# Quantised stage of a three-layer kernel: squares kept in the gelu's low half, and both streams' first rows turned before the first product

## The reference, cut to what matters

```python
def _qlora_linear(x, q, scale, bias, la, lb):
    w = _dequant(q, scale)
    base = jnp.einsum('btd,od->bto', x, w) + bias
    lora = jnp.einsum('btr,or->bto', jnp.einsum('btd,rd->btr', x, la), lb)
    return base + lora
h = x
for blk in range(3):
    i0, i1 = (2 * blk, 2 * blk + 1)
    y = _qlora_linear(h, qweights[i0], scales[i0], biases[i0], lora_a[i0], lora_b[i0])
    y = _layernorm(y, ln_gamma[blk], ln_beta[blk])
    y = jax.nn.gelu(y, approximate=False)
    y = _qlora_linear(y, qweights[i1], scales[i1], biases[i1], lora_a[i1], lora_b[i1])
    h = y + h
...
x = _layernorm(x + _L0_ffn_ref(x, ...), axis=-1)
```

## Time and profile before

| | us |
|---|---|
| median of 3 runs | 2350.44 (2347.72 to 2354.53) |
| the profiled execution, its own time | 2346.15 |
| its span, first to last instruction | 2344.4 |
| mean granted TensorE clock in it | 0.985 |

### The profile page before, as it was taken

The page is one execution under the profiler, slowest core; times in us unless marked ns, Lnnn a source line. Parts: engine busy times, 40 slices in busy tenths (PEclk is TensorE's granted clock), DMA queues, the critical chain, the costliest instruction groups (busy, mean ns, idle before and its releaser), DMA issues.

```text
span 2344.4 us, 35695 instructions
## 1 busy us (share of the span) xinstructions
PE 2249.4 (96%) x11839; PEld 1876.6 (80%) x11839; DVE 1494.6 (64%) x2746; ACT 1277.6 (54%) x2449; POOL 693.6 (30%) x993
## 2 busy tenths in 40 slices
PE   7999999998699999999999999999999999999997
PEld 6999999997578777778787787877877788888886
DVE  3666666676565665666666567566566766666666
ACT  4455555555545354354463444535445577777775
POOL 2565555665100100101001010010010235555555
PEclk9999999998899999999999999999999999999999
DMA  5122221235101102002011020110210423333322
GB/s 146 55 99 89 98 104 51 103 136 155 59 1 55 54 1 90 18 18 72 18 54 54 18 72 18 54 54 0 89 49 19 160 73 108 107 107 107 107 90 72
DMA packets 101704, 166.12 MB, mean 71 GB/s; under 512 B 19664, under 2 KB 22480, under 8 KB 101520
## 3 DMA queue, kind: packets, MB, share of 16 engines
q1 hardware_dynamic: 97328, 163.69, 20.5%
q10 hardware_dynamic: 4320, 1.71, 0.3%
HBM read 115.05 MB, written 50.33 MB: 71 GB/s over the span
## 4 chain that ended last, share of the span: by engine, by line
PE 52%; DVE 11%; ACT 5%; DMA 3%; issue 2%; POOL 1%; DVEq 0%; POOLq 0%; ACTq 0%
PE quant_bank L2002 6%; PE quant_bank L2004 6%; PE quant_bank L2003 6%; PE quant_bank L1631 5%; PE quant_bank L1632 4%; PE quant_bank L1633 4%; PE quant_bank L1661 3%; PE quant_bank L1662 3%; PE quant_bank L1663 3%; DMA x_d<-quant_y 3%; DVE quant_g_lo L1551 2%; DVE quant_h_lo L1512 2%; PE quant_bank L1682 2%; PE quant_bank L1684 2%; PE quant_bank L1683 2%
## 5 line engine op out<-in xcount | busy, mean ns | idle before, releaser
L1429 POOL TENSOR_TENSOR quant_up_rstd<-quant_up_var,quant_minus_half 128x4 f32<-128x4 f32 x48 | 48.6, 1012 | 916.5 <-DVE quant_up_var L1539 916.5
L1631 PE MATMUL quant_bank<-quant_h_hi,kept_W_hi 128*128 128x512 f32 x768 | 308.0, 401 | 7.1 <-DVE quant_h_lo L1512 7.1
L1632 PE MATMUL quant_bank<-quant_h_hi,kept_W_lo 128*128 128x512 f32 x768 | 304.3, 396 | 0.0
L1633 PE MATMUL quant_bank<-quant_h_lo,kept_W_hi 128*128 128x512 f32 x768 | 304.2, 396 | 0.0
L1468 ACT ACTIVATE quant_y<-quant_bank,quant_b_root 128x512 f32<-128x512 f32 x192 | 127.3, 687 | 296.1 <-DMA x_d<-quant_y 158.3
L1967 DVE TENSOR_TENSOR mlp_g_lo<-quant_bank,mlp_g_hi 128x512 fp32r<-128x512 f32 x256 | 176.4, 689 | 106.8 <-ACT quant_bank L1904 106.7
L1903 ACT ACTIVATE mlp_g_hi<-quant_bank,mlp_b 128x512 fp32r<-128x512 f32 x256 | 177.4, 693 | 71.6 <-PE quant_bank L2004 63.7
L1661 PE MATMUL quant_bank<-quant_g_hi,kept_W_hi 128*128 128x512 f32 x512 | 209.0, 408 | 0.0
L1662 PE MATMUL quant_bank<-quant_g_hi,kept_W_lo 128*128 128x512 f32 x512 | 203.6, 398 | 0.0
L1663 PE MATMUL quant_bank<-quant_g_lo,kept_W_hi 128*128 128x512 f32 x512 | 203.3, 397 | 0.0
L1525 DVE TENSOR_TENSOR quant_y<-quant_y 128x512 f32<-128x512 f32 x96 | 66.5, 693 | 212.5 <-ACT quant_y L1468 211.5
(11 more groups left out here) (309 smaller groups left out, 5846.9 us busy)
## 6 DMA issues: line engine op xcount, KB each, us to landing
delta_x_in<-L_attn_x_d SPq DMA_DIRECT2D x16, 1024.0 KB, 8.2
delta_x_res<-L_attn_x_d SPq DMA_DIRECT2D x16, 1024.0 KB, 5.6
x_d<-delta_z SPq DMA_DIRECT2D x64, 256.0 KB, 2.1
quant_y<-x_d SPq DMA_DIRECT2D x16, 1024.0 KB, 5.1
x_d<-quant_y SPq DMA_DIRECT2D x16, 1024.0 KB, 4.2
mlp_x_in<-x_d SPq DMA_DIRECT2D x16, 1024.0 KB, 10.3
mlp_x_res<-x_d SPq DMA_DIRECT2D x16, 1024.0 KB, 6.6
out_d<-mlp_z SPq DMA_DIRECT2D x15, 1024.0 KB, 8.7
```

Source lines behind the costliest of these rows:

```text
L1631: mm(tr[j][:, :], W_hi[2 * b][:, k, cols], h_hi[m][:, k, :], start=k == 0, stop=False)
L1632: mm(tr[j][:, :], W_lo[2 * b][:, k, cols], h_hi[m][:, k, :], start=False, stop=False)
L1633: last = mm(tr[j][:, :], W_hi[2 * b][:, k, cols], h_lo[m][:, k, :], start=False, stop=k == KT - 1)
```

## The change

Three things are changed, all in the quantised layer.

1. The squares get a place of their own, `sq[m]`, which is the memory of `g_lo[m]`. `square`, `part` and both `total` pieces use it instead of `y[m]`. The wait for `x_out` moves from ACT's `square` to DVE's `normed`, the first piece that now writes `y[m]` in a step.
2. In step 0 all `enter` pieces, of both streams, come first on every engine. Stream 1's rows go into the three `lin` banks and `shared` (`first_banks`), so they don't wait for stream 0's `normed`; `up` of stream 1 waits for it instead. The first `total` on PE and the first `down` wait for stream 1's `h_lo`, since they write those banks.
3. ACT's work on the biases moves from the start of the layer to behind the eighth `enter`, with `y[1]` as scratch, and DVE waits for it only before the first `normed`.

```diff
+        sq = [placed(nc, f"quant_sq{m}", [P, KT, R], F32, g_at + (2 * m + 1) * size_of([P, KT, R])) for m in range(STREAMS)]
...
+        first_banks = lin + [shared]
...
-            for what, m, b, i, behind in order:
+            first_enters = several("enter", 0, 0, KS) + several("enter", 1, 0, KS)
+            for what, m, b, i, behind in first_enters + [piece for piece in order if piece not in first_enters]:
...
+        def ahead(t, m):
+
+            return isinstance(t, int) and (t, m) == (0, 1)
+
+        def enters_in(t, m):
+
+            return first_banks if ahead(t, m) else tr
...
+            def centred_biases():
...
-                nc.scalar.activation(h_hi[m][:, k, :], tr[k][:, :], ACT.Copy).then_inc(s["h_hi_done"], 1)
+                nc.scalar.activation(h_hi[m][:, k, :], enters_in(t, m)[k][:, :], ACT.Copy).then_inc(s["h_hi_done"], 1)
+                if isinstance(t, int) and (t, m, k) == (0, 1, KT - 1):
+                    centred_biases()
...
-                if b == 0 and j == 0:
-                    wait(act, s["x_out"], 16 * t)
-                nc.scalar.activation(y[m][:, j, :], tr[j][:, :], ACT.Square, bias=b_root[:, b, j:j + 1], scale=ROOT).then_inc(s["sq_done"], 1)
+                nc.scalar.activation(sq[m][:, j, :], tr[j][:, :], ACT.Square, bias=b_root[:, b, j:j + 1], scale=ROOT).then_inc(s["sq_done"], 1)
...
-            dve.wait_ge(b_done, 2 * BLOCKS)
...
-                nc.vector.tensor_tensor(y[m][:, 0, :], y[m][:, 0, :], y[m][:, j, :], ALU.add).then_inc(s["part_done"], 1)
+                nc.vector.tensor_tensor(sq[m][:, 0, :], sq[m][:, 0, :], sq[m][:, j, :], ALU.add).then_inc(s["part_done"], 1)
...
                     dve.wait_ge(s["row_done"], BLOCKS * t + b + 1)
+                    if b == 0:
+                        wait(dve, s["x_out"], 16 * t)
+                        if isinstance(t, int) and (t, m) == (0, 0):
+                            dve.wait_ge(b_done, 2 * BLOCKS)
...
-                else:
+                elif not ahead(t, m):
                     pe.wait_ge(S[0]["normed"], KT * BLOCKS * t + k + 1)
...
-                if 0 in ks and m == 1 and b > 0:
+                if 0 in ks and m == 1 and (b > 0 or ahead(t, m)):
                     pe.wait_ge(S[0]["normed"], KT * (BLOCKS * t + b) + j + 1)
...
                 pe.wait_ge(s["sum_done"], BLOCKS * t + b + 1)
+                if isinstance(t, int) and (t, m, b) == (0, 0, 0):
+                    pe.wait_ge(S[1]["h_lo_done"], KT)
...
                     lin_free(pe, t, "down", m, b, j)
+                    if isinstance(t, int) and (t, m, b) == (0, 0, 0):
+                        pe.wait_ge(S[1]["h_lo_done"], KT)
```

More of the change, by code:

```diff
@@ L1446, in _ @@
         def _(act):
[L1447 to L1454, removed]
+            def centred_biases():
+                for b in range(BLOCKS):
+                    nc.scalar.activation(y[1][:, b, :], b_all[:, b, :], ACT.Copy, scale=-1.0 / dim, accum_out=b_mean[:, b:b + 1]).then_inc(b_done, 1)
+                act.wait_ge(b_done, BLOCKS)
+                for b in range(BLOCKS):
+                    nc.scalar.activation(b_mid[:, b, :], b_col[:, 2 * b, :], ACT.Identity, bias=b_mean[:, b:b + 1]).then_inc(b_done, 1)
+                act.wait_ge(b_done, 2 * BLOCKS)
+                nc.scalar.activation(b_root[:, :, :], b_mid[:, :, :], ACT.Copy, scale=ROOT).then_inc(b_done, 1)
+                act.wait_ge(b_done, 2 * BLOCKS + 1)
             def enter(t, m, b, k):
@@ L1516, in enter @@
                     dve.wait_ge(S[m]["xT_ps"], KT * t + KT)
-                split_h(t, m, 0, k, tr[k][:, :])
+                split_h(t, m, 0, k, enters_in(t, m)[k][:, :])
             def part(t, m, b, j):
@@ L1532, in total @@
                 dve.wait_ge(s["part_done"], 2 * u + 2)
-                nc.vector.scalar_tensor_tensor(y[m][:, 0, :], y[m][:, KT - 1, :], LN_EPS / P, y[m][:, 0, :], ALU.add, ALU.add).then_inc(s["sum_done"], 1)
+                nc.vector.scalar_tensor_tensor(sq[m][:, 0, :], sq[m][:, KT - 1, :], LN_EPS / P, sq[m][:, 0, :], ALU.add, ALU.add).then_inc(s["sum_done"], 1)
             def spread(t, m, b, _):
@@ L1613, in enter @@
                     wait(pe, S[1]["normed"], KT * (BLOCKS * t - 1) + k + 1)
-                else:
+                elif not ahead(t, m):
                     pe.wait_ge(S[0]["normed"], KT * BLOCKS * t + k + 1)
                 for r in range(RT):
-                    last = nc.tensor.transpose(tr[k][:, r * P:(r + 1) * P], arrived(t, m)[:, r, k * P:(k + 1) * P], ident)
+                    last = nc.tensor.transpose(enters_in(t, m)[k][:, r * P:(r + 1) * P], arrived(t, m)[:, r, k * P:(k + 1) * P], ident)
                 last.then_inc(s["xT_ps"], 1)
@@ L1639, in total @@
                 pe.wait_ge(s["sum_done"], BLOCKS * t + b + 1)
+                if isinstance(t, int) and (t, m, b) == (0, 0, 0):
+                    pe.wait_ge(S[1]["h_lo_done"], KT)
                 for r in range(RT):
-                    last = nc.tensor.transpose(by_rows[:, r, :], y[m][:, 0, r * P:(r + 1) * P], ident)
+                    last = nc.tensor.transpose(by_rows[:, r, :], sq[m][:, 0, r * P:(r + 1) * P], ident)
                 last.then_inc(s["sum_ps"], 1)
```

## The result

| | before | changed |
|---|---|---|
| median us | 2349.08 (4 runs, 2347.04 to 2354.53) | 2310.68 (4 runs, 2310.04 to 2311.67) |
| ratio, 95% interval | | 0.9833 (0.9816 to 0.9851) |
| span of the profiled execution | 2344.4 | 2309.9 |

The changed kernel is faster by 1.7%: 38.4 us by these medians, 34.5 us by the two profiled spans. A second set of 19 runs of the kernel before gave 2347.49, 36.8 us above the changed kernel. The forecast was 2313 in 2305 to 2322.

The account below looks back on a forecast made before the run. PE, busy 96% of the span, was taken as the bound. Gains 27.6 + 4.5 + 3.4 - 0.4 = 35.1 us gave 2311.1 from the profiled 2346.15, or 2315.3 from the median; forecast 2313, range 2305 to 2322.

Parts of the forecast that it names:

- What bounds the kernel: Whole kernel: PE is busy 96% of the span, so other engines' waits count only as far as they reach PE.
- The stalls: PE at `total`, 14 places in steps 1 to 7: idle time and pipe filling all go, 27.6 us, lower bound 20.6.
- the clock behind them: PE behind three of the stalls: stretches at the lower clock go, 1.5 us each, 4.5 us; lower bound 0.
- the new wait: DVE ahead of the first `normed` of a step: the added wait instruction costs 0.03 us each, 0.4 us in 14.
- the halfway correction: Forecast time: median runs 4.3 us above the profiled execution; the middle of 2311.1 and 2315.3 was taken, 2313.
- The moved wait: DVE's `normed`, step 1: the store lands before DVE needs it, 7.0 us to spare for stream 0, some 6 for stream 1.
- The first pass: Step 0: `up` of stream 1 starts 3.4 us earlier (bounds 2.2 and 3.9), `up` of stream 0 1.3 us later.
- a term set at nothing: Step 0, `up` of stream 1: slow matmuls at 1.2 GHz before and after set against each other, 1.5 us either way.
- moving the biases: ACT, start of the quantised layer: biases end near 626.5, ahead of the first square; moving them costs nothing.
- part of the stall stayed: Rival, PE at `total`: DVE's sum comes late, 19 us gained, 2327 to 2331; chance 0.05.
- other wait took its place: Rival: PE waits elsewhere for the same time, only the first pass gained, 2343 to 2347; chance 0.02.
- The one that ends slower: Rival, DVE's `normed`: stores landing beyond 11.2 us hold it; gain eaten up at 13.7 us, 2366 at 15; chance 0.03.

Follow-up runs that it names:

- the wait back: Changed kernel with only the wait for the store put back on ACT's first square of a step and taken from DVE, squares staying in `g_lo`: 2345.64 us.
- squares alone: Kernel before with only the squares moved to `g_lo` and the store wait on DVE's `normed`; order and first pass as before: 2314.08 us.
- biases first: Changed kernel with ACT's nine bias instructions back ahead of its first `enter` copy, DVE's early wait staying away: 2310.67 us.
- the store after the fourth square: Changed kernel with each store of steps 0 to 6 issued only after the fourth square of the next step's first block: 2310.39 us.
- The delayed stores: Changed kernel with stores of steps 0 to 6 held until the next step's fourth square, `total` or `spread`: 2310.39, 2315.47, 2361.36 us.
- the first pass alone: Changed kernel with squares, sums and the store wait back in `y`, keeping the new first pass and moved biases: 2344.44 us.
- the stores held back to `spread`: Changed kernel with each store of steps 0 to 6 issued only after PE's `spread` of the next step's first block: 2361.36 us.

## Why the prediction was right

**What bounds the kernel.** The reading held. 158.3 us of ACT's wait were worth 33 us, because only what reached PE counted: the kernel with the wait back has ACT's wait and PE's, and is as slow as before.

**The stalls, 27.6 us, and the clock behind them, 4.5 us, less 0.4 for the new wait.** Together 31.7; the stretch with the seven steps is 32.5 us shorter, and squares alone gave 33.4 between medians. Of the 32.5, 24.7 us are PE's idle time at `total`, as read the earlier trace rows, and 7.8 are what the prediction had as pipe filling and clock, 7.4. The clock of 0.87 and 0.88 behind three of the stalls is gone: the window of the changed kernel from 700 to 1740 us reads 1.00. That every stall would go was argued from two rows where `total` had no wait; the distance at the same place is now 0.59 us, like the 0.60 of the unstalled block. That the clock term varies between runs is borne out by the runs: 19 of the kernel before spread over 9.4 us, the fastest (2342.89) at a mean granted clock of 0.989, the slowest (2352.32) at 0.983. Twelve runs without the stalls, of the changed kernel, of biases first and of the store after the fourth square, spread over 3.0 us (2309.16 to 2312.11). The price of 1.5 us for each stretch was read at one of the three; the other two have fewer slow matmuls (5 and 6, not 8). The step "the median of before lies above its profile, and that difference goes too" was a choice between 2311.1 and 2315.3; the sum made against the profiled execution, 2311.1, was the better one, and the halfway correction an addition that the result didn't need. The range's gain of 29 to 39 us was narrower than the bounds set for the terms (20.6 for the stalls and 0 for the clock at the low end), so that the measured gain lies inside it says little for the low end.

**The moved wait.** Put at 7.0 us to spare for stream 0 and some 6 for stream 1. In step 1 of the changed kernel the stores land 7.1 and 5.3 us before `normed` (773.38 + 4.17 against 784.65, 800.02 + 5.11 against 810.43). The delayed stores bear out the size: nothing lost at 4.6 us, 4.8 us at about 6.6. Stream 1 has the less room, because its `normed` follows a `down` and came 810.43 - 803.60 = 6.8 us after the last matmul of `up`, where stream 0's came 784.65 - 776.85 = 7.8 after it; the prediction had used stream 0's distance for both. The term of 0.4 us for the wait instruction itself was a guess that no row of before showed, and it didn't reach PE. On DVE it can be read: from the end of ACT's `rstd_row` to the first `normed` of stream 0 it is 0.13 to 0.14 us in steps 1 to 7, where the kernel before has 0.03; for stream 1 it is 0.03 in both.

The section from which the prediction takes its 4.4 us for a store (the Trainium skill, DMA: Bandwidth & Descriptors, "Anatomy of one DMA — SWDGE (gpsimd) path") is about transfers issued from GpSimd. These stores are issued from SyncE, so that they land in 4.2 us at the median is no test of it. The rule that a transfer's completion can come surprisingly late when its target is HBM (the Trainium skill, Perfetto Trace Analysis, "DMA Instruction — HWDGE (DVE, Sync)") did not show here: the stores land in 4.1 to 5.1 us in the changed kernel.

**The first pass, 3.4 us.** 3.2 in the trace, 3.1 between medians without the squares and 3.4 with them, but that the sum behind it came out was partly luck. `up` of stream 1 starts 22.79 us into the layer where it started at 27.12, 4.3 us earlier, since `up` of stream 0 came only 0.7 us later (5.11 for 4.45), not 1.3: about half of the 32 transposes started 0.21 us apart, as all 16 had before, and the other half 0.11 us apart, which makes some 1.8 us for the second sixteen where 2.3 had been taken. Against that stands a term set at nothing, with 1.5 us either way: 13 matmuls of that `up` ran at 1.2 GHz, where it had been 7. Before, 16 transposes had run in the slow stretch ahead of the matmuls; now the matmuls themselves, which are longer, are in it. Six more, 0.2 us each, are 1.2 us. This varies too: the seven traces with the new first pass up to the delayed stores have 9 to 13 such matmuls. That moving the biases would cost and give nothing held exactly (2310.67 for 2310.68).

**The rivals.** No part of the stall stayed, and no other wait took its place. The one that ends slower is real: held back by about 10 us the stores make the kernel slower than before. Its break-even had been put at a landing 9.5 us later than now (13.7 for 4.2), with nothing lost up to 7. By that count about 10 us would lose 14 x 3 = 42 us; they lost 50.7, against the 37 gained, so the break-even lies a little lower. The count left out the clock that falls behind such waits and the smaller room of stream 1; that it came near is partly luck, since not each late microsecond of DVE reaches PE either (67.2 us of DVE's wait for 50.7 lost).

## What to carry to other kernels

A long wait of an engine off the critical path is to be priced by the bounding engine's own wait behind it, plus the filling of its pipe (0.2 us here, each time) and the clock it may lose; the wait's own length says nothing. Look in the trace for a place where the same piece already runs without the wait, a first iteration or another block: it shows whether the whole stall goes and what is next. When a buffer is shared between a slow store and a computation, move only the first use out of it into memory that is dead then, and measure the room left by delaying the store, not by trusting one profile.

## What the runs showed of the hardware

The lower clock comes after short idle times, and not after all of them. In the profiled executions of the kernel before, of the first pass alone and of the wait put back, PE had 42 stalls at `total` in steps 1 to 7. Of the 38 that lasted 1.37 to 1.99 us, 6 (1.83 to 1.91 us) were followed by 5 to 8 matmuls at 1.2 GHz, and others as long were not; of the other four (2.17, 2.63, 2.64 and 3.40 us), all were. With the stores held back to `spread`, all seven idle times of 2.41 to 2.47 us, each closely preceded by one of 0.86 to 1.74, were followed by it, and in each case 7 to 12 matmuls ran slow. So two stalls of nearly the same length in the same loop differ in cost by about 1.2 us (six matmuls 0.2 us further apart). The stalls can thus make the kernel before scatter more between runs than the changed one; that they are the whole difference was not shown, since only profiled executions tell which stall was followed by slow matmuls.
